# Two table stores moved from GpSimd's DMA queue to SyncE's, and three register instructions less, in a two-layer graph network kernel

## The reference, cut to what matters

```python
def _L0_gnn_ref(x, edge_index, W, att_src, att_dst, bias):      # H = 4, C = 256
    xp = (x @ W).reshape(N, H, C)
    e = leaky_relu(a_src[src] + a_dst[dst], 0.2)                # a_src, a_dst: xp . att_src, att_dst
    alpha = segment_softmax(e, dst)
    return relu(segment_sum(xp[src] * alpha, dst).reshape(N, H * C) + bias)

def _L1_gnn_ref(x, edge_index, rms_w, W_down, Wl, Wr, att, W_up):   # HID = 256, H = 4
    x = rmsnorm(x) * rms_w @ W_down
    xl, xr = x @ Wl, x @ Wr
    e = (leaky_relu(xl[src] + xr[dst], 0.2) * att).sum(-1)      # per head
    alpha = segment_softmax(e, dst)
    return segment_sum(alpha * xl[src], dst) @ W_up

x = layernorm(x + L0(x)); x = layernorm(x + L1(x))
```

## Time and profile before

| | |
|---|---|
| runs | 2469.5, 2473.44, 2473.68 us; median 2473.44 |
| profiled execution | 2469.5 us, its span 2467.8 us |
| busy share of the span | PE 77%, PEld 51%, DVE 64%, ACT 35%, POOL 61% |
| DMA | 544.13 MB, mean 220 GB/s |
| queue q0 (issued by GpSimd) | 275.43 MB |
| queue q1 (issued by SyncE) | 240.51 MB |

### The profile page before, as it was taken

The page is one execution under the profiler, slowest core; times in us unless marked ns, Lnnn a source line. Parts: engine busy times, 40 slices in busy tenths (PEclk is TensorE's granted clock), DMA queues, the critical chain, the costliest instruction groups (busy, mean ns, idle before and its releaser), DMA issues. The chain is left out here.

```text
span 2467.8 us, 50665 instructions
## 1 busy us (share of the span) xinstructions
PE 1902.7 (77%) x10665; PEld 1256.4 (51%) x10666; DVE 1584.2 (64%) x3964; ACT 870.1 (35%) x2928; POOL 1501.3 (61%) x1567
## 2 busy tenths in 40 slices
PE   4869888888258888888867984777777773999687
PEld 2534444433146666566646773555555552676533
DVE  5324333333487666666659985666656668999877
ACT  1300000000057777777756763000000002555355
POOL 2077777777767777777751116777777763666410
PEclk9979999999579999999988997999999996999899
DMA  6343333333249999999989964888888881777577
GB/s 231 111 155 83 87 90 80 80 80 76 82 148 359 362 359 358 354 364 359 355 303 312 315 232 126 245 237 240 246 231 249 230 239 53 245 256 252 187 224 225
DMA packets 257401, 544.13 MB, mean 220 GB/s; under 512 B 54394, under 2 KB 144771, under 8 KB 257292
## 3 DMA queue, kind: packets, MB, share of 16 engines
q0 software_dynamic: 99904, 275.43, 34.3%
q1 hardware_dynamic: 138118, 240.51, 29.9%
q10 hardware_dynamic: 19302, 27.36, 4.0%
HBM read 453.73 MB, written 102.38 MB: 225 GB/s over the span
## 5 line engine op out<-in xcount | busy, mean ns | idle before, releaser
L928 ACT ACTIVATE wone<-onehot,w 128x64 f32<-128x64 f32 x1760 | 432.2, 334 | 137.0 <-DVE onehot L972 130.8
L148 POOL DMA_INDIRECT acc<-xl_table,csrc x392 | 400.2, 1021 | 125.3 <-issue 105.2
L148 POOL DMA_INDIRECT ga<-a_src_table,csrc x392 | 392.4, 1001 | 121.3 <-issue 102.2
L820 PE MATMUL banks<-w_sb,xT 128*128 128x512 f32 x800 | 383.7, 630 | 57.7 <-DVE xp_st L862 44.4
L945 PE MATMUL banks<-rows,wone 128*64 128x256 f32 x2368 | 316.2, 392 | 64.0 <-DMA rows<-xp_table,isrc 34.4
L148 POOL DMA_INDIRECT rows<-xp_table,isrc x296 | 294.8, 996 | 90.7 <-issue 53.0
L968 DVE TENSOR_TENSOR acc<-banks,acc 128x512 f32 x440 | 304.3, 692 | 2.4 <-issue 0.6
L1399 PE MATMUL banks<-xr_parts,onehot_t 128*128 x1320 | 188.3, 286 | 131.0 <-issue 102.2
L820 PEld LDWEIGHTS banks<-w_sb,xT 128*128 128x128 f32 x800 | 151.5, 200 | 215.5 <-issue 199.5
L1399 PEld LDWEIGHTS banks<-xr_parts,onehot_t 128*128 128x128 bf16 x1320 | 127.4, 96 | 215.2 <-issue 175.8
L1427 DVE SCALAR_TENSOR_TENSOR prod<-banks,att_relu 128x1024 f32<-128x1024 f32 x110 | 134.7, 1224 | 157.4 <-ACT w L1364 154.6
(11 more groups left out here) (259 smaller groups left out, 2895.0 us busy)
## 6 DMA issues: line engine op xcount, KB each, us to landing
edge_rows<-acc SPq DMA_DIRECT2D x440, 130.0 KB
rows<-edge_rows SPq DMA_DIRECT2D x55, 1040.0 KB, 4.9
xin<-in_x SPq DMA_DIRECT2D x48, 512.0 KB, 7.7
lt_bc<-local_dst SPq DMA_DIRECT2D x110, 128.0 KB, 3.5
lt<-local_dst ACTq DMA_DIRECT2D x110, 128.0 KB
xp_table<-xp_st SPq DMA_DIRECT2D x25, 512.0 KB, 2.9
w<-acc SPq DMA_DIRECT2D x100, 128.0 KB, 4.0
xpt<-xp_table SPq DMA_DIRECT2D x25, 512.0 KB, 5.3
```

Of the source, the lines that this page charges most:

```text
L148: return self.pool.indirect_dma_start(out, None, table, bass.IndirectOffsetOnAxis(ap=idx, axis=0), bounds_check=self.bound, oob_is_err=False)
L820: last = nc.tensor.matmul(psum[:, 2 + i], xT[:, k, :], w_sb[:, k, i * 512:(i + 1) * 512], start=(k == 0), stop=(k == KD - 1))
L928: last = nc.scalar.activation(wone[:, s, j, h, :], onehot[:, s, j, :], ACT.Copy, scale=w9[:, bass.ds(g * U + j, 1), h:h + 1].rearrange("p ...
```

## The change

The two stores of the node stage leave GpSimd and are issued by SyncE, in the same `pipelined` list as the loads and after them, with lags of 4 and 7 turns in place of 3 and 6. Their waits become plain waits of SyncE. GpSimd keeps only its three memsets in this block. The number, size, source and target of the DMAs stay as they are. In both logits stages the maximum with 0 goes.

```diff
@@ VectorE, logits of layer one
                         dve.reg_alu(last_group, chunks.regs[U - 1], 2, ALU.logical_shift_right)
-                        dve.reg_alu(last_group, last_group, 0, ALU.max)
                         dve.wait_ge(s_fetched, dve.snap(last_group, min_val=0, max_val=NGC - 1) + 1)
@@ GpSimd, node stage
-                    order = PoolGather(pool, N, bound)
-
-                    def store_x1(t, s, m):
-                        s2, m2, s3, m3 = slots(s, m)
-                        order.wait(S["x1"], t + 1)
-                        pool.dma_start(x1_t[bass.ds(t * P, P), :], y[:, s3, :]).then_inc(s_x1s[s3], 16)
-
-                    def store_xl(t, s, m):
-                        s2, m2, s3, m3 = slots(s, m)
-                        order.wait(S["sf"], t + 1)
-                        pool.dma_start(xl_t[bass.ds(t * P, P), :], xls[:, s2, 0:XLW]).then_inc(s_xls[s2], 16)
-                    pipelined(pool, NT, [(3, store_x1), (6, store_xl)], AHEAD, 6)
@@ SyncE, node stage
-                    pipelined(sp, NT, [(0, load_sums), (0, load_weights), (0, load)],
+                    def store_x1(t, s, m):
+                        s2, m2, s3, m3 = slots(s, m)
+                        sp.wait_ge(S["x1"], t + 1)
+                        sp.dma_start(x1_t[bass.ds(t * P, P), :], y[:, s3, :]).then_inc(s_x1s[s3], 16)
+
+                    def store_xl(t, s, m):
+                        s2, m2, s3, m3 = slots(s, m)
+                        sp.wait_ge(S["sf"], t + 1)
+                        sp.dma_start(xl_t[bass.ds(t * P, P), :], xls[:, s2, 0:XLW]).then_inc(s_xls[s2], 16)
+                    pipelined(sp, NT, [(0, load_sums), (0, load_weights), (0, load), (4, store_x1), (7, store_xl)],
                               AHEAD, 6)
@@ SyncE, logits of layer two
                         sp.reg_alu(last_group, chunks.regs[U - 1], 2, ALU.logical_shift_right)
-                        sp.reg_alu(last_group, last_group, 0, ALU.max)
@@ TensorE, logits of layer two
                         pe.reg_alu(last_group, chunks.regs[U - 1], 2, ALU.logical_shift_right)
-                        pe.reg_alu(last_group, last_group, 0, ALU.max)
```

## The result

The changed kernel takes 2489.74 us (the median of six runs, which go from 2486.28 to 2492.65) against 2472.18 us for six runs of the kernel before, the three shown above and three more. The ratio is 1.0074, with a 95% interval of 1.0063 to 1.0084: it is 17.6 us slower, where the forecast was 2476 (+2.1 by the sum), and 0.7 us above the top of the range. The profiled execution took 2489.01 us, its span is 2487.2 us.

The account below looks back on a forecast made before the run. VectorE was taken to set the node stage's pace, with the DMA engines close behind. Start +3.0, steady turns +1.8, DRAIN -2.2 and registers -0.5 summed to +2.1 us, 2475.5 against the median, rounded to 2476; range 2468 to 2489.

Parts of the forecast that it names:

- What becomes tight is the landing: Node stage: combine(v-1) overwrites the y slot of tile v-4 and waits until that tile's x1 store has landed.
- the formula for the turn: Node stage: a turn lasts the larger of 7.2 us and (D+4.6)/2.
- D: When the x1 store lands, counted from the turn's start; taken as +10.0, giving 0.1 us over some 18 turns, 1.8 us.
- rival (a): Node stage: the store lands late, D +10.6 to +11.4, turns of 7.6 to 8.0 us, 2481 to 2490 us; chance 0.34.
- the start: Node stage's first turns: x1(0) stands behind load(4), so combine(3) and the turns after are delayed; 3.0 us lost (2 to 4.5).
- the registers: Maximum with 0 dropped in both logits stages: 38 ns per group, hidden except on TensorE; 0.5 us gained.
- the lower end: Landing estimate from the last stage, where SyncE's queue works alone: xpt at +7.2, xin +8.5, x1 +9.8.
- the DRAIN: Node stage's end: without DMAs of its own POOL is done early and the barrier follows SyncE; 2.2 us gained.
- rival (c): Node stage's end: the barrier keeps its tail, so the 2.2 us stay; 2478 us; chance 0.04.
- with that cover gone: SyncE's issue of both stores, hidden behind its 3.5 us wait for VectorE's statistics, would otherwise cost 1.1 us a turn.
- The new waits hold nothing up: SyncE's waits for x1 and xl delay no load: VectorE makes both before the statistics SyncE awaits anyway.
- Rival (b): Node stage: nothing waits and loads come sooner; -2.7 to -9.8 us, 2464 to 2471 us; chance 0.18.

Follow-up runs that it names:

- e15: Both stores moved to SyncE without the register change, the x1 store issued ahead of xpt and xin; against the kernel before: ratio 1.0034.
- e5: Both stores on SyncE, x1 store a turn earlier (lag 3), xl store between sum loads and xpt, maxima kept; against the kernel before: ratio 0.9987.
- e8: Only the stage's last three x1 and last two xl stores moved to SyncE, behind its last load; against the kernel before: ratio 0.9980.
- e10: e2 with the last xin load cut into 48 and 5 rows; against the kernel before: ratio 1.0048.
- e7: e2 with three slots for xls in place of two; against the kernel before: ratio 1.0080.
- e16: e15 with three slots for xls in place of two; against the kernel before: ratio 1.0005.
- e4: Only the xl store moved to SyncE (lag 7), x1 store left with GpSimd, maxima kept; against the kernel before: ratio 1.0014.
- e1: Stores left with GpSimd, one register instruction less in each of three places (one AND for shift and maximum); against the kernel before: ratio 1.0007.
- e3: Only the x1 store moved to SyncE (lag 4), xl store left with GpSimd, maxima kept; against the kernel before: ratio 1.0089.
- e2: Both stores moved to SyncE as in the changed kernel, but the maxima kept; against the kernel before: ratio 1.0080.
- e14: e2 with the x1 store one turn later (lag 5); one run, 2640.47 us.

## Why the prediction was wrong

**The mechanism was right, and the sum chose its milder case.** "What becomes tight is the landing", the formula for the turn, and "it decides from D = +10.4 on" all held; the time is at the upper end of rival (a), which said D of +10.6 to +11.4, turns of 7.6 to 8.0 us and 2481 to 2490 us. The trace has landings at +10.6 on average and turns of 7.71 us, both near the rival's lower end; that the time is at its upper end comes from the start and the end of the stage. By parts the profile shows +4.9 for the start (forecast +3.0), +8.2 for the turns behind it (+1.8), +2.4 for the end (-2.2), and no gain from the registers (-0.5).

**The term that was mis-sized is D, "I take +10.0, nearer the lower end".** It was priced at 1.8 us over 18 turns, and 16 turns cost 8.2. The store landed at +10.6 on average, and combine started 0.3 us behind the landing, which had no price: together +10.9. The lower end came from a stage where a 512 KB load lands in 4.3 us and the next transfer 1.3 us later. Here xpt lands in 4.8 us, which with its issue is +7.6 instead of +7.2, and xin at +9.3 instead of +8.5. Ahead of xpt stand four sum loads, 512 KB in SyncE's own queue, and the chain left them out; with the x1 store right behind the sums it landed in 3.9 us (e15). That the sums are what was missing is argued from these two, not shown. The argument that a longer turn relieves the queue was true (xin 6.0 us, from 8.0), but it was used twice: the lower end already came from a relieved queue. Above +9.8 half of each microsecond is paid in every turn, so these 0.9 us cost 0.4 us a turn beyond the 0.1 that was priced.

**The Trainium skill's rule** (DMA: Bandwidth & Descriptors, section "Issuing engines are not separate DMA queues"), by which the store would land as long after its issue as before, pointed to the right case, but its size did not come: 6.5 us instead of 7.5, at +10.6 on average instead of +11.4. e5 agrees with it further: with all stores in SyncE's queue the turn is 7.06 us, beside 7.02 with two queues.

**The start** was forecast at 3.0 us (2 to 4.5); the four turns from load(4) to load(8) lost 4.9. The first step was right, and the turns behind it were priced too low. The rows are the store of x1(0) and the combines of tiles 3 and 4.

```profile
1316.71 0.43 SPq L1071 DMA_DIRECT2D x_table<-y  x1
...
1323.30 1.67 DVE L1225 SCALAR_TENSOR_TENSOR y<-xpt,sw,w 128x256 f32<-128x256 f32 x4 [1.00 <-issue]
...
1331.23 0.88 DVE L1225 SCALAR_TENSOR_TENSOR y<-xpt,sw,w 128x256 f32<-128x256 f32 x2 [2.42 <-issue]
```

x1(0) lands in 6.5 us, at 1323.2, and combine(3) starts 2.3 us later in the stage than before, where 2.0 to 2.6 was said. Combine(4) waits 2.42 us more, above the 1 to 2 us of the turns behind it.

**The end was missing from the sum, but for the DRAIN.** That term held: 2.4 us of gap became 0.2, and did so too in e8, where most stores stayed with GpSimd, so rival (c) is out. But "with that cover gone" was asked only of SyncE's issue time, not of the last load, which showed a stretch of one engine's work (share 0.06, 25 GB/s) and a wait of 1.5 us already in the trace of before. Putting the x1 stores behind that load cost 6.8 us of waiting at one place, and apart from the barrier's gain the stage's end lost 4.6 us. e10 took some 8 us off by moving 5 rows into a DMA of their own.

**"The new waits hold nothing up"** held for SyncE's waits on semaphores. The xl store's own landing was priced only for the last tile: in the changed kernel ScalarE waits 25.9 us for it. That costs nothing there (e7), but it does cost when combine's wait is gone (e15 against e16) and when the xl store moves alone (e4, 3.5 us).

**The registers** were priced at -0.5 us, with a fused instruction 38 ns shorter on TensorE; it is 18 ns shorter, and e1 shows no gain.

**Rival (b)** (nothing waits and the loads come sooner) is what e5 shows, but with only 2.8 us at the median (0.9987): it needed the store a turn earlier.

The profiled turns of e3 (7.94 us) are longer than those of e2 (7.69), with less in SyncE's queue. This needs no cause in the kernel: e10, with the code of e2 up to its last load, has 7.90, and the intervals of e2 and e3 overlap. What makes single landings differ, from +9.7 to +11.4 in the changed kernel, stays open.

## What to carry to other kernels

When a store moves behind loads in a queue, count from the event that releases it to the event that needs its buffer, over how many turns that loop closes, and put every transfer ahead of it in the queue into its landing; beyond the point where the loop closes, a microsecond of landing is paid once per round of the loop: half a microsecond a turn when it closes over two turns, a whole one when it closes over one. Look at the odd-sized last transfer too: the one of 53 rows kept a single DMA engine busy, and what stood behind it waited for it. Removing one wait does not tell what the next one costs: a slot that was free of charge behind the first wait costs when that is gone.

## What the runs showed of the hardware that was not expected

A load of 53 rows of 4 KB occupies one of 16 DMA engines (share 0.06, 26 GB/s) for some 8 us, and 512 KB stores issued behind it land 13.1 us after their issue instead of 6.5; with 48 and 5 rows they land in 5.9 and 6.3. GpSimd's DRAIN at the node stage's end takes 3.3 us (e3), 4.0 us (e4, e8) and 4.7 us (before) behind DMAs of its own, and without any it ends with GpSimd's last memset; it opened the barrier late only where GpSimd issued its last DMA late (before, e3). A wait that this profile books as "issue" can be a wait for a DMA's landing: of two neighbouring turns of e14 with the same 8.1 us one was booked so and one to the store, and both waits ended just behind a landing.
